# Causal cross-attention with its four groups of 512 queries overlapped, one product for the queries, and the mask, row sums and division moved

## The reference, cut to what matters

```python
def _L1_xattn_ref(enc_outputs, x, Wq):
    q = jnp.einsum('bld,hd->blh', x, Wq)
    k = jnp.einsum('bld,hd->blh', enc_outputs, Wq)
    v = k
    scores = jnp.einsum('bqh,bkh->bqk', q, k) / jnp.sqrt(jnp.float32(d_k))
    causal = jnp.tril(jnp.ones((Lq, Lk), dtype=bool))
    scores = jnp.where(causal, scores, -jnp.inf)
    attn = jax.nn.softmax(scores, axis=-1)
    return jnp.einsum('bqk,bkh->bqh', attn, v)
...
x = x + _L1_xattn_ref(ctx_1024, _layernorm(x, axis=-1), L1_xattn_Wq)
```

## Time and profile before

| | us |
|---|---|
| median of 3 runs | 2907.46 |
| lowest and highest run | 2895.34, 2909.18 |
| the profiled execution, its own time | 2903.92 |
| its span, first to last instruction | 2902.1 |

### The profile page before, as it was taken

How to read it: one execution, slowest core, us unless ns; L and a number is a source line. 1 busy time by engine, 2 the same in 40 slices (tenths; PEclk the granted TensorE clock), 3 DMA queues, 4 the chain that set the end, 5 groups by cost and what they waited for, 6 DMA issues and landing times. The chain is left out here.

```text
span 2902.1 us, 74278 instructions
## 1 busy us (share of the span) xinstructions
PE 2535.6 (87%) x31022; PEld 1708.5 (59%) x31022; DVE 1931.2 (67%) x6301; ACT 1407.3 (48%) x2596; POOL 435.2 (15%) x304
## 2 busy tenths in 40 slices
PE   7998854798999999999999999999969998988544
PEld 5776643455777556666666666666645555665423
DVE  5554413576311478888888888888588885556776
ACT  3442311465334345555555555555469953334521
POOL 1000022342000100000000000000008930753200
PEclk9998876899899989999999999999789999999866
DMA  7970231000000100000000100000012211990000
GB/s 238 332 271 11 81 93 32 8 3 18 8 22 15 43 25 25 31 31 25 25 25 25 36 25 25 25 25 14 2 41 94 89 37 65 355 353 19 2 0 15
DMA packets 73374, 189.52 MB, mean 65 GB/s; under 512 B 12130, under 2 KB 39717, under 8 KB 73008
## 3 DMA queue, kind: packets, MB, share of 16 engines
q1 hardware_dynamic: 64912, 156.68, 16.4%
q10 hardware_dynamic: 7104, 26.23, 2.5%
q0 software_dynamic: 1024, 1.85, 0.2%
HBM read 154.19 MB, written 30.79 MB: 64 GB/s over the span
## 5 line engine op out<-in xcount | busy, mean ns | idle before, releaser
L3174 DVE CUSTOM_DVE_ANT_0 L_xattn_junk<-L_xattn_ps_mx,L_xattn_shift 128x512 f32<-128x512 f32 (+1 forms) x1024 | 544.7, 569 | 140.0 <-issue 139.0
L3245 ACT ACTIVATE L_xattn_pT<-L_xattn_ps_st 128x512 f32<-128x512 f32 x768 | 417.1, 595 | 352.2 <-PE L_xattn_ps_st L3002 231.1
L3017 PE MATMUL L_xattn_ps_mx<-L_xattn_kT,L_xattn_qb 32*128 32x512 f32 (+1 forms) x2048 | 513.9, 554 | 1.2 <-DVE L_xattn_tops L3174 1.2
L3002 PE MATMUL L_xattn_ps_st<-L_xattn_qb,L_xattn_kT 32*128 32x256 f32 (+1 forms) x3328 | 471.4, 383 | 0.0
L3212 DVE TENSOR_TENSOR L_xattn_pT<-L_xattn_pT,L_xattn_capT 128x1024 f32<-128x1024 f32 (+1 forms) x325 | 362.1, 1115 | 18.3 <-ACT L_xattn_pT L3245 15.9
L3002 PEld LDWEIGHTS L_xattn_ps_st<-L_xattn_qb,L_xattn_kT 32*128 32x128 f32 (+1 forms) x3328 | 340.9, 185 | 7.0
L3067 PE MATMUL L_xattn_ps_pv<-L_xattn_pT,L_xattn_v 128*17 128x128 f32 x6656 | 266.9, 280 | 0.0
L3067 PEld LDWEIGHTS L_xattn_ps_pv<-L_xattn_pT,L_xattn_v 128*17 128x17 f32 x6656 | 150.8, 98 | 144.4 <-issue 114.4
L3017 PEld LDWEIGHTS L_xattn_ps_mx<-L_xattn_kT,L_xattn_qb 32*128 32x128 f32 x2048 | 169.3, 185 | 32.0 <-DVE L_xattn_tops L3174 27.1
L3029 PE MATMUL L_xattn_ps_st<-L_xattn_less,L_xattn_ones_b 3*128 3x512 bf16 x768 | 187.6, 390 | 0.5 <-ACT L_xattn_pT L3245 0.5
L2940 POOL TENSOR_TENSOR L_xattn_qb<-ln_sq,L_xattn_four 128x256 f32<-128x256 f32 x32 | 20.6, 645 | 993.8 <-PE L_xattn_ps_st L3002 989.1
(11 more groups left out here) (626 smaller groups left out, 4941.7 us busy)
## 6 DMA issues: line engine op xcount, KB each, us to landing
L_xattn_ctxT<-context_turned SPq DMA_DIRECT2D x64, 800.5 KB, 6.8
context_turned<-L_xattn_ctxT SPq DMA_DIRECT2D x32, 800.5 KB, 9.4
L_xattn_ctx<-in_ctx SPq DMA_DIRECT2D x32, 768.0 KB
L_xattn_ctx<-in_ctx ACTq DMA_DIRECT2D x32, 768.0 KB
L_attn_cc<-scratch_rows SPq DMA_DIRECT2D x32, 512.0 KB, 3.7
L_xattn_out_keys<-scratch_q SPq DMA_DIRECT2D x32, 200.1 KB, 10.0
L_ffn_w<-in_L_ffn_w SPq DMA_DIRECT2D x4, 1024.0 KB, 10.5
L_ffn_w<-in_L_ffn_W SPq DMA_DIRECT2D x16, 256.0 KB, 3.1
```

Of the source, the lines that this page charges most:

```text
L3002: last = nc.tensor.matmul(st[0:chunk[j], w % 3, 256 * c2:256 * c2 + 256], kT[n % 3][r:r + 32, P * j:P * j + chunk[j]], qb[n % 3][r:r + 32, ...
L3017: last = nc.tensor.matmul(mx[:, w % 3, to:to + width], qb[n % 3][32 * g:32 * g + 32, 2 * (p % 2):2 * (p % 2) + 2, :].rearrange("p h q -> p ...
L3174: last = nc.vector.tensor_tensor_reduce(out=junk[:, w % 3, to:to + width], in0=mx[:, w % 3, to:to + width], in1=shift[:, k0:k0 + width], s ...
L3245: nc.scalar.activation(pT[b % HELD][:, :, gi, :], st[:, w % 3, :].rearrange("p (c k) -> p c k", c=2), ACT.Exp)\
```

## The change

The layer's program is rewritten; the norm's ScalarE helper gets hooks, so that steps of the layer can stand between its own.

- **Keys.** They are used where they land (`keys`, all 16 tiles); the copy at L767 is gone. All 16 transposes run between the norm's, into four banks that are free then (`turned_keys`), and are copied to `keysT`, two groups by ScalarE and two by VectorE. TensorE waits for `loaded` after the norm's second set of transposes. SP issues `w`, the keys, `mask`, `wT` in that order.
- **Queries.** TensorE forms `w`·`w` once (128 x 128); ScalarE scales it into `square`. A group then needs one product with 512 columns instead of two with a VectorE copy between them.
- **Mask.** It is the first product into the bank of scores (bf16 identity by bf16 mask, 512 columns), to which the score products add.
- **Softmax.** VectorE takes the row maxima from PSUM and negates them; ScalarE reads the scores from PSUM in four pieces of 128 columns with the negated maximum as bias and adds up the rows. The division is left to the last step, four VectorE instructions that multiply by the reciprocal and add `x`.
- **Overlap.** The banks of queries, scores and transposes, and the tiles `qk`, `sc`, `probsT`, `oT`, are doubled, and the order on each engine is written by hand so that a group's steps stand between those of the group before.

```diff
@@ ln_scalar
-def ln_scalar(c, act, V, A, PE, tp, n=None):
+def ln_scalar(c, act, V, A, PE, tp, n=None, between=None):
...
         last.then_inc(A.did(f"{g}_xn{i}"), 1)
+        if f"xn{i}" in between:
+            between[f"xn{i}"]()
...
@@ causal_cross_attention
+        mask, mask_b, ident_b = s.sb("mask", [P, P]), s.sb("mask_b", [P, P], BF16), s.sb("ident_b", [P, P], BF16)
+        keys = s.sb("keys", [P, NT, D])
+        keysT = s.sb("keysT", [P, G, 512])
+        square = s.sb("square", [P, D])
+        qk = s.sb("qk", [P, 2, 512])
+        sc, probsT, oT = (s.sb(n, [P, 2, 4, P]) for n in ("sc", "probsT", "oT"))
+        mx, neg, rows, rinv = (s.sb(n, [P, NT]) for n in ("mx", "neg", "rows", "rinv"))
+        turn, pqk, psc = (s.ps(n, [P, 2, 512]) for n in ("turn", "qk", "sc"))
...
+        turned_keys = [psc[:, 0, :], psc[:, 1, :], po[:, :], pout[:, :]]
...
             sp.dma_start(w[:, :], a[f"{name}_Wq"]).then_inc(loaded, 16)
-            sp.dma_start(wT[:, :], a[f"{name}_WqT"]).then_inc(loaded, 16)
-            sp.dma_start(mask[:, :], a["c_pair_causal"]).then_inc(loaded, 16)
             for b in (0, 1):
                 src = a["ctx"].rearrange("(t b) k d -> b k t d", b=2)[b, 0:S, :, :]
-                sp.dma_start(keys_all[S * b:S * b + S, :, :], src).then_inc(loaded, 16)
+                sp.dma_start(keys[S * b:S * b + S, :, :], src).then_inc(loaded, 16)
+            sp.dma_start(mask[:, :], a["c_pair_causal"]).then_inc(loaded, 16)
+            sp.dma_start(wT[:, :], a[f"{name}_WqT"]).then_inc(loaded, 16)
...
         @block.tensor
+            def turn_keys(g):
+                for i in range(4):
+                    last = nc.tensor.transpose(turned_keys[g][:, P * i:P * i + P], keys[:, 4 * g + i, :], c.ident[:, :])
+                last.then_inc(PE.did(f"keysT{g}"), 1)
+            def between_turns(i):
+                if i == 1:
+                    pe.wait_ge(loaded, 80)
+                    nc.tensor.matmul(pqk[:, 0, 0:D], w[:, :], w[:, :], start=True, stop=True).then_inc(PE.did("square"), 1)
+                    turn_keys(0)
+                    turn_keys(1)
+                elif i == 2:
+                    turn_keys(2)
+                    turn_keys(3)
+            def queries(g):
+                if g >= 2:
+                    pe.wait_ge(*A.at(f"qk{g - 2}"))
+                nc.tensor.matmul(pqk[:, (g + 1) % 2, :], square[:, :], c.xnT[:, 512 * g:512 * g + 512], start=True, stop=True)\
+                    .then_inc(PE.did(f"qk{g}"), 1)
+            def scores(g):
+                pe.wait_ge(*A.at(f"qk{g}"))
+                if g >= 2:
+                    pe.wait_ge(*A.at(f"exp{g - 2}"))
+                else:
+                    pe.wait_ge(*V.at("keysT2"))
+                    pe.wait_ge(*V.at("keysT3"))
+                nc.tensor.matmul(psc[:, g % 2, :], ident_b[:, :], mask_b[:, :].unsqueeze(1).broadcast_to([P, 4, P]), start=True, stop=False)
+                for i in range(4):
+                    last = nc.tensor.matmul(psc[:, g % 2, P * i:P * i + P], qk[:, g % 2, P * i:P * i + P], keysT[:, g, P * i:P * i + P],
+                                            start=False, stop=(i == 3))
+                last.then_inc(PE.did(f"scores{g}"), 1)
+            def mix(g):
+                pe.wait_ge(*A.at(f"exp{g}"))
+                if g >= 2:
+                    pe.wait_ge(*A.at(f"probsT{g - 2}"))
+                for i in range(4):
+                    last = nc.tensor.transpose(tp[g % 2][:, P * i:P * i + P], sc[:, g % 2, i, :], c.ident[:, :])
+                last.then_inc(PE.did(f"probsT{g}"), 1)
+                pe.wait_ge(*A.at(f"probsT{g}"))
+                if g >= 1:
+                    pe.wait_ge(*V.at(f"oT{g - 1}"))
+                for i in range(4):
+                    last = nc.tensor.matmul(po[:, P * i:P * i + P], keys[:, 4 * g + i, :], probsT[:, g % 2, i, :], start=True, stop=True)
+                last.then_inc(PE.did(f"oT{g}"), 1)
+            def result(g):
+                pe.wait_ge(*V.at(f"oT{g}"))
+                if g >= 1:
+                    pe.wait_ge(*V.at(f"x{g - 1}"))
+                for i in range(4):
+                    last = nc.tensor.matmul(pout[:, P * i:P * i + P], oT[:, g % 2, i, :], wT[:, :], start=True, stop=True)
+                last.then_inc(PE.did(f"out{g}"), 1)
+            ln_tensor(c, pe, V, A, PE, tp, between=between_turns)
+            pe.wait_ge(*A.at("square"))
+            pe.wait_ge(*A.at("ln_T1"))
+            queries(0)
+            queries(1)
+            pe.wait_ge(*A.at("keysT1"))
+            scores(0)
+            queries(2)
+            scores(1)
+            queries(3)
+            mix(0)
+            scores(2)
+            result(0)
+            mix(1)
+            scores(3)
+            result(1)
+            mix(2)
+            result(2)
+            mix(3)
+            result(3)
         @block.vector
+            for g in (2, 3):
+                dve.wait_ge(*PE.at(f"keysT{g}"))
+                nc.vector.tensor_copy(keysT[:, g, :], turned_keys[g]).then_inc(V.did(f"keysT{g}"), 1)
+            def largest(g, first, second):
+                at = slice(4 * g, 4 * g + 4)
+                dve.wait_ge(*PE.at(f"scores{g}"))
+                nc.vector.tensor_reduce(mx[:, at], four(psc[:, g % 2, :]), AX.X, ALU.max).then_inc(V.did(first), 1)
+                dve.wait_ge(*V.at(first))
+                nc.vector.tensor_scalar(neg[:, at], mx[:, at], -1.0, None, ALU.mult).then_inc(V.did(second), 1)
+            largest(0, "max0", "neg0")
+            largest(1, "max1", "neg1")
+            for g in range(G):
+                dve.wait_ge(*A.at(f"exp{g}"))
+                nc.vector.reciprocal(rinv[:, 4 * g:4 * g + 4], rows[:, 4 * g:4 * g + 4]).then_inc(V.did(f"rinv{g}"), 1)
+                dve.wait_ge(*PE.at(f"oT{g}"))
+                if g >= 2:
+                    dve.wait_ge(*PE.at(f"out{g - 2}"))
+                nc.vector.tensor_copy(oT[:, g % 2, :, :], four(po[:, :])).then_inc(V.did(f"oT{g}"), 1)
+                if g < 2:
+                    largest(g + 2, f"next_max{g}", f"next_neg{g}")
+                dve.wait_ge(*V.at(f"rinv{g}"))
+                dve.wait_ge(*PE.at(f"out{g}"))
+                for i in range(4):
+                    t = 4 * g + i
+                    last = nc.vector.scalar_tensor_tensor(out=c.x[:, t, :], in0=pout[:, P * i:P * i + P], scalar=rinv[:, t:t + 1],
+                                                          in1=c.x[:, t, :], op0=ALU.mult, op1=ALU.add)
+                last.then_inc(V.did(f"x{g}"), 1)
         @block.scalar
+            def after_copies(i):
+                if i == 1:
+                    act.wait_ge(*PE.at("square"))
+                    nc.scalar.activation(square[:, :], pqk[:, 0, 0:D], ACT.Copy, scale=D ** -0.5).then_inc(A.did("square"), 1)
+                    nc.scalar.copy(mask_b[:, :], mask[:, :]).then_inc(A.did("mask_b"), 1)
+            def turned(g):
+                act.wait_ge(*PE.at(f"keysT{g}"))
+                nc.scalar.copy(keysT[:, g, :], turned_keys[g]).then_inc(A.did(f"keysT{g}"), 1)
+            def queries(g):
+                act.wait_ge(*PE.at(f"qk{g}"))
+                if g >= 2:
+                    act.wait_ge(*PE.at(f"scores{g - 2}"))
+                nc.scalar.copy(qk[:, g % 2, :], pqk[:, (g + 1) % 2, :]).then_inc(A.did(f"qk{g}"), 1)
+            def exps(g):
+                act.wait_ge(*negated(g))
+                if g >= 2:
+                    act.wait_ge(*PE.at(f"probsT{g - 2}"))
+                for i in range(4):
+                    t = 4 * g + i
+                    last = nc.scalar.activation(sc[:, g % 2, i, :], psc[:, g % 2, P * i:P * i + P], ACT.Exp, bias=neg[:, t:t + 1], scale=1.0,
+                                                accum_out=rows[:, t:t + 1])
+                last.then_inc(A.did(f"exp{g}"), 1)
+            def probabilities(g):
+                act.wait_ge(*PE.at(f"probsT{g}"))
+                if g >= 2:
+                    act.wait_ge(*PE.at(f"oT{g - 2}"))
+                nc.scalar.copy(probsT[:, g % 2, :, :], four(tp[g % 2])).then_inc(A.did(f"probsT{g}"), 1)
+            nc.scalar.copy(ident_b[:, :], c.ident[:, :]).then_inc(A.did("ident_b"), 1)
+            ln_scalar(c, act, V, A, PE, tp, between={"T1": lambda: after_copies(1), "xn2": lambda: turned(0), "xn3": lambda: turned(1)})
+            queries(0)
+            queries(1)
+            exps(0)
+            queries(2)
+            probabilities(0)
+            exps(1)
+            queries(3)
+            probabilities(1)
+            exps(2)
+            probabilities(2)
+            exps(3)
+            probabilities(3)
```

91 lines of the change are left out of this document (14 added, 77 removed).

## The result

| | before | after |
|---|---|---|
| median, us | 2906.56 (4 runs) | 2860.91 (4 runs) |
| lowest and highest run | 2895.34, 2909.18 | 2853.66, 2868.02 |
| the profiled execution, its own time | 2903.92 | 2865.53 |
| its span | 2902.1 | 2863.7 |
| the layer, from its first transfer's issue to the next layer's | 80.64 | 39.61 |

The ratio is 0.9844, 95% interval 0.9823 to 0.9866. The kernel became faster by 1.6%; 2864 had been predicted, with a layer 39.9 us shorter, and in the profiles it is 41.0 us shorter.

What follows compares the result with a forecast made beforehand. It took the layer to be bound by a serial chain through the engines, no engine full. Head to 474.0, then opening, mixing, slots and tail less joints end it at 499.5, not 539.4: 2903.9 - 39.9 = 2864 us, range 2853 to 2880.

Steps and rivals of the forecast that it cites:

- serial rival: Layer's body: the groups do not overlap, the chain stays serial, only shorter; 13.9 us per group, 2894 us; chance 0.07.
- The head: Layer's start to first query product: waiting for keys until 467.3, first query product at 474.0, a loss of 4 us.
- the late rise: Head: TensorE idle before the landing, so its clock may rise some 3.5 us later; first query product then at 475.0.
- The body: From the first query product at 474.0 to the layer's end at 499.5, TensorE working through its new list.
- The opening: Start of the body: four query products and two score sets on TensorE, 7.3 us, to 481.3.
- mixing: After the opening: the first group's transposes 0.63, copy 0.59 and two hand-overs of 0.04; 1.3 us, to 482.6.
- two slots: Mid-body: products with keys, a later group's scores, last products, next transposes, copy and hand-overs; 5.03 us each, 10.1 together.
- the tail: End of the body, where nothing is left to overlap: remaining products, transposes, copies and final VectorE instructions; 8.7 us, to 501.4.
- the joint: Body on TensorE: the next work hides a row's tail, 0.16 us; twelve such joints take 1.9 us off the sum.
- The low clock: Rival: TensorE stays at or falls to 1.2 GHz; 18 us if throughout the body, some 5 if partly; 2869 to 2882; chance 0.21.
- The transfers: Rival in the norm's wait: each microsecond of landing after 467.3 costs one; slower only if 54 us later; chance 0.02.
- warning signs: Transposes waiting for exponentials; clock 0.50 after 480; a landing wait beyond 468.5; score rows clearly longer than 1.5 us.

Runs made afterwards that it cites:

- the serial rival's kernel: Changed kernel with its four groups one after another on every engine, nothing else altered; 2890.83 us against 2907.33 for the kernel before, ratio 0.9935.

## Why the prediction was right, step by step

**The mechanism** was the chain and its overlap, and it held: the serial rival's kernel, built as such, came out at 2890.8 where 2894 had been worked out, and the order was worth the difference. That its group took 13.95 us where the sum had 13.9 is luck in part. The sum ended a group with the adding into `x`, for which the next query product does not wait, and with this the way from the last products to that product was priced 1.4 us too long; query product and scores, priced at the upper level, ran at the lower one, and the way from them to the transposes was priced 1.5 us too short.

**The head** was predicted to reach the first query product 14.95 us after the layer's start and took 15.04, but by two errors that cancel, which is luck. The landing was taken at 8.25 us after the start, with 9.45 as its upper end, and came at 9.5. Half of that is a misread row. Of the two issues of keys in the earlier trace rows the prediction gave the longer time to landing, 7.4, to the first; it is the second's. In the kernel before, the keys landed at 461.4 + 7.4 = 468.8, and not at 467.8 at the latest, with 1.2 us to spare before 470.04 and not over 2. That is 9.7 us after the start; less the prediction's own 0.9 us for the earlier issue it is 8.8, and they came at 8.9. The other 0.6 us are the small transfers: the issue of the mask, 0.43 us in its place before, took 1.38 behind the keys, and `wT` was waited for in vain. The 2.35 us of idleness were followed by 3.4 us at the lower level. Against that, what follows the landing had been priced by whole rows at 5.4 us at the upper level, 6.7 with the late rise; it took 475.87 - 470.38 = 5.5 us, most of it at the lower level. Its rows run into each other: at the upper level a set of four transposes starts 0.43 us behind the one ahead of it (474.56, 474.99), not 0.63.

**The body** was priced at 25.5 us and took 500.16 - 475.87 = 24.3. The opening took 5.94 where the sum, with its joints, had 6.5; mixing 1.27 for 1.3; two slots 4.26 and 4.28 for 4.55; the tail 8.54 for 8.54. So the term that was mis-sized in the body is the joint. It was taken as 0.16 us, from one row. In the slot the next row starts 0.99, 0.89 and 0.89 us after the three sets of products, each priced at 1.16, and in the opening the next row starts 0.86 us after a query product, priced at 1.12: a joint between rows is worth 0.17 to 0.27. In the tail, where waits stand between the rows, the sum had a single joint, which measured 0.16, and there is no error.

**What was new in form:** the exponentials took 1.50 us per group, predicted 1.7; four ACTIVATEs of 357 to 383 ns, each 0.35 us after the last, with the accumulator's read in between. The Trainium skill (ScalarE: Activation LUTs, "What ACT_TABLE_LOAD costs") led to an estimate of 387 ns each, next start after 294; the trace's lengths are at most 8% below it, and its pitch, with the read in between, is longer. The mask product occupies 0.22 us, predicted 0.25. Adding scores to its bank costs nothing, as taken: 1.05 for eight records. The identity's cast was hidden, and the table load of 1.28 too.

**The rivals.** The low clock did not come in the body, where it had its price, but it did in the head, behind a gap of 2.35 us. In the serial kernel, with gaps of at most 2.5 us, it was low for most of the body, where the prediction had pointed to the old kernel's 4.55 as what it takes. The bound was too comfortable: with the first group's transposes 1.25 us later the clock fell inside the body as well, and took 1.7 us of a slot. The transfers were late by 1.3 us beyond what was taken, not 54.

**The signs named in advance.** In the slots the waits before the products are on the copy only, 0.68 us each; the transposes of later groups wait for nothing; the clock is at 1.00 from 474.5. One of the warning signs was there, if barely, a landing beyond 468.5 (9.5 us after the start against 9.45), and cost less than the body's joints gave back.

**The time.** 2903.9 - 39.9 = 2864 stood for the profiled execution, which gave 2865.53. The medians, 2860.9 and 2855.6, lie below it, and the long layer's clock, of which the prediction says nothing, explains that as far as the bands of runs do. So the layer's gain was worked out, and what the medians gained beyond it was not.

## What to carry to other kernels

Where a chain through three engines leaves TensorE idle for most of a period, price the overlap twice: once as the overlap, and once as the clock that it keeps up; here the two were worth the same, 15.7 and 15.1 us. A wait placed in the middle of an in-order list stops all that is behind it: the same transfers, waited for one step later and in a smaller number, made the layer 2.6 to 3.5 us shorter. And when runs of one kernel fall into two bands, find the layer that differs before crediting a change with the gap.
